# Mixture-of-experts stage of a Trainium2 kernel: experts' products of the first half of the tokens, two tiles at a time, among the projections of the second half

## The reference, cut to what matters

```
xn = layernorm(x)
logits = xn @ gate_w.T                          # 8 experts
scores = softmax(logits); weights, idx = top_k(scores, 2)
base = xn @ W_lin.T + b_lin                     # 256 -> 256
t = einsum('nd,nkdr->nkr', xn, left[idx])       # rank 4 per expert
lora = sum_k weights * einsum('nkr,nkro->nko', t, right[idx])
x = x + base + lora
```

## Time and profile before

| what | value |
|---|---|
| median of 3 runs | 5746.22 us (5745.38 to 5751.06) |
| the profiled execution: time, span | 5745.98 us, 5744.2 us |
| ffn0 | about 2289 to 2366 us of the span |
| ffn1 | about 5672 us to the end |
| PE, DVE, ACT busy over the whole span | 71%, 82%, 78% |
| granted PE clock over the whole span | 0.821 of full speed |

### The profile page before, as it was taken

One profiled execution on the slowest core, in us unless ns is written; L12 is line 12 of the kernel. 1 busy time (PEld: TensorE's weight loads), 2 busy tenths in 40 slices (PEclk: granted clock), 3 DMA queues, 4 the chain that ended last, 5 costly groups with the idle time before them and its releaser, 6 DMA issues. The chain is left out here.

```text
span 5744.2 us, 68969 instructions
## 1 busy us (share of the span) xinstructions
PE 4105.5 (71%) x22020; PEld 1826.6 (32%) x22020; DVE 4724.3 (82%) x7143; ACT 4453.8 (78%) x3416; POOL 1435.7 (25%) x1260
## 2 busy tenths in 40 slices
PE   8999999999999998855555555555555555555547
PEld 4555555555555555611111110111011111111105
DVE  7666666766666666699999999999999999999966
ACT  4555555555555555559999999999999999999994
POOL 0000000000000000034444444444444444444320
PEclk9999999999999999966667677767766676667668
DMA  1000000000000000279998989899999999999881
GB/s 40 5 6 5 5 5 5 5 5 5 5 5 5 6 6 1 79 175 189 186 198 186 198 185 198 186 198 186 197 187 198 186 198 186 198 186 198 184 193 63
DMA packets 149377, 639.49 MB, mean 111 GB/s; under 512 B 32662, under 2 KB 74840, under 8 KB 79064
## 3 DMA queue, kind: packets, MB, share of 16 engines
q0 software_dynamic: 73728, 536.90, 46.6%
q1 hardware_dynamic: 75224, 97.37, 5.1%
HBM read 70.22 MB, written 27.13 MB: 17 GB/s over the span
## 5 line engine op out<-in xcount | busy, mean ns | idle before, releaser
L1500 DVE SCALAR_TENSOR_TENSOR b_tiles<-b_ra_rep,b_cap,psum 128x1024 f32<-128x1024 f32 x1024 | 1261.0, 1271 | 56.4 <-PE psum L1761 54.1
L1761 PE MATMUL psum<-b_qT,b_kT 126*128 126x512 bf16 x2048 | 815.8, 509 | 683.7 <-DVE b_tiles L1500 680.4
L679 DVE CUSTOM_DVE_ANT_0 a_srow<-psum,a_bias 128x512 f32<-128x512 f32 (+3 forms) x1280 | 725.6, 607 | 497.6 <-PE psum L860 494.5
L738 ACT ACTIVATE a_pT<-psum 128x512 f32<-128x512 f32 (+3 forms) x1056 | 511.6, 527 | 661.0 <-PE psum L872 660.7
L1774 PE MATMUL psum<-b_tiles,b_v_aug 128*32 128x512 f32 x2752 | 524.8, 849 | 485.8 <-ACT b_tiles L1675 485.8
L1507 DVE TENSOR_SCALAR b_tiles<-b_tiles 128x2048 f32<-128x2048 f32 x512 | 767.3, 1499 | 4.4
L872 PE MATMUL psum<-ident,a_srow 128*128 128x128 f32 x4352 | 625.7, 280 | 70.5 <-DVE a_pT L551 32.9
L1666 ACT ACTIVATE b_tiles<-b_tiles 128x4096 f32<-128x4096 f32 x172 | 613.1, 3610 | 19.9 <-DVE b_tiles L1106 19.0
L756 ACT ACTIVATE a_srow<-a_srow,a_nmax 128x1536 f32<-128x1536 f32 (+15 forms) x512 | 610.3, 1197 | 23.1 <-DVE a_nmax L685 21.2
L1761 PEld LDWEIGHTS psum<-b_qT,b_kT 126*128 126x128 bf16 x2048 | 156.6, 110 | 1474.1 <-DVE b_tiles L1500 1115.2
L860 PE MATMUL psum<-a_k,a_q 64*128 64x512 f32 (+3 forms) x2560 | 624.7, 573 | 0.0
(11 more groups left out here) (221 smaller groups left out, 5242.0 us busy)
## 6 DMA issues: line engine op xcount, KB each, us to landing
b_tiles<-b_tiles POOLq DMA_DIRECT2D x344, 1024.0 KB, 13.1
X<-b_tiles POOLq DMA_DIRECT2D x168, 1024.0 KB, 13.1
b_ra_rep<-ra_scratch SPq DMA_DIRECT2D x32, 1024.0 KB, 9.9
row_scratch<-b_tiles SPq DMA_DIRECT2D x6, 2048.0 KB, 16.2
b_qk_raw<-row_scratch SPq DMA_DIRECT2D x31, 304.0 KB, 2.8
b_v_raw<-row_scratch SPq DMA_DIRECT2D x31, 136.0 KB, 8.6
X<-in_x_dram SPq DMA_DIRECT2D x8, 512.0 KB, 6.6
a_wqk<-in_wqk_dram SPq DMA_DIRECT2D x32, 128.0 KB, 2.6
```

The source lines that it names most:

```text
L679: nc.vector.tensor_tensor_reduce(out=srow[:, n % ROWS, h, a:z], in0=bank(c % 2 * 2 + h, 0, z - a), in1=bias[:, h, off + a:off + z], scale= ...
L1500: nc.vector.scalar_tensor_tensor(out=a[:, s * HALF:(s + 1) * HALF], in0=ra_rep[:, j, s * HALF:(s + 1) * HALF], scalar=cap[:, j, k:k + 1], ...
L1761: last = nc.tensor.matmul(half_ps(s)[:, i * BANK:(i + 1) * BANK], kT[:, j, k * P:(k + 1) * P], qT[:, j, cs], start=True, stop=True)
```

## The change

With HN = 8, the results n = 0 to 7 of the first half are made one by one inside the projection loop: from tile LEFT_AT = 24 on, PE issues `left_of_two(t - 24)` and `right_of_two(t - 25)` after the tile's own work, ACT copies 256 columns instead of 512, and DVE adds result t - 26 after its own work for the tile. The five parts of `choose(0)` move to the tiles 16, 17, 19, 21 and 23, and ACT's exponential to tile 16. To make room in PSUM, `joint` rotates over three banks instead of four; `left_of_two` has a bank of its own (6) and `right_of_two` two (5 and 7). The tail keeps `left` and `right` for q = 4 to 7 only, and these wait for the second half's `tl` and for the eight additions of the first half. `right_of_two(7)`, and the additions 6 and 7, stand behind the loop (the additions behind `choose(1)` too).

```diff
         def ps_joint(t, a, b):
-            return env.psum[:, (2 + t % 4) * BANK + a:(2 + t % 4) * BANK + b]
+            return env.psum[:, (2 + t % 3) * BANK + a:(2 + t % 3) * BANK + b]
...
         def ps_lora(n):
-            return env.psum[:, (2 + n % NL) * BANK:(3 + n % NL) * BANK]
+            i = (5, 7)[n % 2] if n < HN else 2 + n % NL
+            return env.psum[:, i * BANK:(i + 1) * BANK]
+        ps_tlT2 = env.psum[:, 6 * BANK:6 * BANK + 2 * P]
+        def lefts(q):
+            return HN + q - NQ // 2 + 1
...
+            def add(n):
+                dve.wait_ge(lora_done, n + 1)
+                dve.wait_ge(base_added, 2 * n + 2)
+                xt = env.X[:, 2 * n:2 * n + 2, :].rearrange("p a d -> p (a d)")
+                nc.vector.tensor_tensor(xt, ps_lora(n), xt, ALU.add).then_inc(x_added, 1)
+                if after is not None:
+                    dve.wait_ge(x_added, n + 1)
+                    after.sums(2 * n)
+                    after.sums(2 * n + 1)
...
-                if t >= HT and t % 3 == 1 and t // 3 - 5 < 5:
-                    choose(0, t // 3 - 5)
+                if t in CHOOSE_AT:
+                    choose(0, CHOOSE_AT.index(t))
+                if 0 <= t - LEFT_AT - 2 < HN:
+                    add(t - LEFT_AT - 2)
             for part in range(5):
                 choose(1, part)
-            dve.wait_ge(base_added, NT)
-            for n in range(2 * NQ):
...
+            for n in range(NT - LEFT_AT - 2, 2 * NQ):
+                add(n)
...
-                if t == HT + 1:
+                if t == HT:
                     exponentials(0)
+                n = t - LEFT_AT
+                if 0 <= n < HN:
+                    act.wait_ge(tlT_done, n + 1)
+                    if n >= 2:
+                        act.wait_ge(lora_done, n - 1)
+                    nc.scalar.activation(tlT[:, n % 2, 0:2 * P], ps_tlT2, ACT.Copy).then_inc(tlT_copied, 1)
             exponentials(1)
-            for q in range(NQ):
-                act.wait_ge(tlT_done, q + 1)
-                if q >= 2:
-                    act.wait_ge(lora_done, (q - 1) * 2)
+            for q in range(NQ // 2, NQ):
+                act.wait_ge(tlT_done, lefts(q))
+                act.wait_ge(lora_done, max((q - 1) * 2, HN))
...
                 pe.wait_ge(xT_copied, t + 1)
-                if t >= 4:
-                    pe.wait_ge(base_added, t - 3)
-                    pe.wait_ge(raw_copied, t - 3)
+                if t >= 3:
+                    pe.wait_ge(base_added, t - 2)
+                    pe.wait_ge(raw_copied, t - 2)
...
+            def left_of_two(n):
+                pe.wait_ge(tl_done, 1)
+                pe.wait_ge(ones_done, 2)
+                if n:
+                    pe.wait_ge(tlT_copied, n)
+                for i in range(2):
+                    last = nc.tensor.transpose(ps_tlT2[:, i * P:(i + 1) * P], tl[:, 2 * n + i, :], env.ident[:, :])
+                last.then_inc(tlT_done, 1)
+            def right_of_two(n):
+                pe.wait_ge(tlT_copied, n + 1)
+                if n >= 2:
+                    pe.wait_ge(x_added, n - 1)
+                for i in range(2):
+                    last = nc.tensor.matmul(ps_lora(n)[:, i * D:(i + 1) * D], tlT[:, n % 2, i * P:(i + 1) * P], ra[:, :],
+                                            start=True, stop=True, skip_group_check=True)
+                last.then_inc(lora_done, 1)
...
                 joint(t)
                 if t + 2 < NT:
                     transpose_x(t + 2)
+                if 0 <= t - LEFT_AT < HN:
+                    left_of_two(t - LEFT_AT)
+                if 0 <= t - LEFT_AT - 1 < HN:
+                    right_of_two(t - LEFT_AT - 1)
+            for n in range(NT - LEFT_AT - 1, HN):
+                right_of_two(n)
...
-            left(0)
-            for q in range(NQ):
-                if q + 1 < NQ and (q + 1) % (NQ // 2):
+            left(NQ // 2)
+            for q in range(NQ // 2, NQ):
+                if q + 1 < NQ:
                     left(q + 1)
                 right(q)
```

More of the change, by code:

```diff
@@ L122, in stage_ffn @@
     HT = NT // 2
+    HN = HT // 2
     NL = 6
+    LEFT_AT = HT + 8
+    CHOOSE_AT = [HT, HT + 1, HT + 3, HT + 5, HT + 7]
     with ExitStack() as ctx:
@@ L325, in left @@
             def left(q):
[L327 to L330, removed]
+                pe.wait_ge(tl_done, 2)
+                pe.wait_ge(tlT_copied, lefts(q) - 2)
                 for i in range(4):
@@ L335, in right @@
             def right(q):
-                pe.wait_ge(tlT_copied, q + 1)
+                pe.wait_ge(tlT_copied, lefts(q))
                 for h in range(2):
                     n = 2 * q + h
-                    if n >= NL:
-                        pe.wait_ge(x_added, n - NL + 1)
+                    pe.wait_ge(x_added, max(n - NL + 1, HN))
                     for i in range(2):
```

## The result

The changed kernel takes 5758.59 us (median of 13 runs, 5755.72 to 5763.58); the kernel before took 5746.3 us (median of 13, 5743.66 to 5751.94). The ratio is 1.0021, with a 95% interval from 1.0013 to 1.0028: it is slower, by 12.3 us. A ratio of 1 lies outside the interval, and the difference is just about the 0.2% that the prediction took for the least that can be told. Forecast were 5759 us. The profiled execution's span is 5756.6 us against 5744.2.

The account below looks back on a forecast made before the run. PE was taken to bound the projection loop. ffn1's tail 7.47, ffn0's tail 2.46 and the clock's 1.9 and 1.4 sum to +13.2 us on 5745.98, 5759.2, stated as 5759; range 5752 to 5764.

Parts of the forecast that it names:

- the price of a tile with products: Projection loop: PE takes 1.00 + 0.22 + 0.22 + 0.87 = 2.31 us for a tile with a left and a right.
- The rival that the products fit in for nothing: Projection loop: PE has room for the products, saving 6.76 us a stage, so the kernel gets faster; chance 0.05.
- Denser choosing: Projection loop: compressed choosing stalls PE for 3.2 us, net +2.6 a stage; with 6.76 for products, `base(31)` is 9.35 later.
- Three banks: Projection loop: `joint` over three banks costs nothing; if wrong, at most 0.3 us a tile.
- Tails: From the loop's end to the last addition: with the loop's delay, ffn1 ends 7.47 us later, ffn0 2.46.
- The clock behind the loop: PE idles during the second choosing, then runs 3 to 6 us at half speed: +1.9 us in ffn1, +1.4 in ffn0.
- The Trainium skill's penalty: PE's clock behind the choosing: throttled time times one half; by it ffn1 would lose 1.7 to 2.8 us.
- B: Rival: PE's clock stays up in one or both waits behind the loop; +9.9 to +11.3 us, 5756 to 5757.5; chance 0.18.
- C: Rival: compressed choosing stalls PE less in the loop; +8 us, or +4.7 without the clock's loss, 5751 to 5754; chance 0.11.
- D: Rival: products fit into the loop for nothing; 5745.7 us, or 5740.5 without the stalls too; chance 0.05.
- E: Rival: ffn0's additions hold up `right_of_two` through `x_added`, or the half-speed stretch lasts longer; over 5764 us; chance 0.04.
- The forecast's account of ffn0: ffn0: six additions (8.3 us) move into DVE's idle time and repay most of the loop's 9.35; end +2.46 without the clock.

Follow-up runs that it names:

- e7: The changed kernel with each of the eight `right_of_two` computed twice into the same place; median 5774.67 us.
- e1: The kernel before with only the denser choosing (`choose(0)` after tiles 16, 17, 19, 21, 23, exponential after tile 16), no product moved; 5748.61 us, ratio 1.0002.
- e6: The changed kernel with the products begun one tile later (LEFT_AT 25), `add(5)` still ahead of choosing; median 5757.82 us.
- e2: The kernel before with `joint` over three PSUM banks instead of four, nothing else; 5746.12 us, ratio 1.0.
- e9: The changed kernel with identity transposes filling PE's waits: 50 ahead of `left(4)`, 8 and 12 in the loop's two stalls; 5756.72 us, ratio 1.0016.
- e5: The changed kernel with 50 identity transposes on PE between `right_of_two(7)` and `left(4)`, filling the wait for the second choosing; 5759.69 us.
- e3: The change in ffn1 alone, ffn0 as in the kernel before; 5758.4 us, ratio 1.0017.
- e11: The changed kernel executed once more, unaltered, for a second profile; 5763.78 us (one run).
- e4: The change in ffn0 alone, ffn1 as in the kernel before; 5750.25 us, ratio 1.0008.
- e8: The kernel before with 44 identity transposes at the start of each mixture stage's PE program; 5743.01 us, ratio 0.9993.
- e10: The kernel before with identity transposes in PE's long waits: 32 at each mixture stage's start, 60 behind ffn0's `right(7)`, 24 at attention B; 5739.52 us, ratio 0.9988.

## Why the prediction was right

The forecast was right in its mechanism and in its sum, 5759 against 5758.59. That the sum hit within 0.4 us is luck: in the profiled executions ffn1 grew by 8.69 us where 9.4 was forecast, ffn0 by 4.26 where 3.9 was, and all the rest fell by 0.6 where nothing was. Step by step:

*What bounds the loop, and the price of a tile with products.* Forecast 2.31 us, measured 2.30, and e7 shows that PE sets it. The rival that the products fit in for nothing has fallen.

*Denser choosing.* Forecast a net 2.6 us, and with the products `base(31)` 9.35 later; measured 9.26 in ffn1 and 9.61 in ffn0. Less 6.76 for the products, 2.5 are left in ffn1. e1 gives 1.0 of them to the density, where 0.9 was forecast, and 1.5 remain for `joint(25)` behind the wait for `tl`, of which e6 takes back 1.2. The 0.35 us that ffn0 has more lie between ACT's `raws(31)` and `base(31)`; what holds DVE there is open. In e6 ffn0 does not have them (25.56 against 25.57).

*Three banks.* Nothing, as forecast (e2).

*Tails.* Without the clock ffn1 was forecast 7.47 us longer; e9 has 46.05 against 38.64, 7.41. In ffn0 2.46 was forecast, and the two parts of it that the clock leaves alone (28.22 to `base(31)` in e9, 23.18 from there in e5) give 51.40, against 48.08: 3.3. The difference is 0.35 as above and 0.50 in which `right(4)` waits for additions 6 and 7 with their sums: the forecast had weighed that wait in ffn1 only.

*The clock behind the loop.* Forecast 1.9 and 1.4 us, measured 1.28 in ffn1 and 0.95 in ffn0 (e5 against the changed kernel). The mechanism was right. The size of ffn1 is one draw: e3 lost 2.31, and the forecast lies between. The Trainium skill's penalty (TensorE: Matmul & The Clock Gate, Terms), half the throttled time, agrees: the clock was at 0.50 for about 3 us after `left(4)` in ffn1, half of which is 1.5, and some of it PE spent waiting; in e3 it was about 5 us, half of which is 2.5, against 2.31. The prediction's own figure by that rule, 1.7 to 2.8, does not follow from its 3 to 6 us, which give 1.5 to 3; nothing in the sum rests on it.

*What was missing.* The clock can also fall in the loop's own stalls, 1.4 to 1.6 us a stage, in half of the stages seen. In the profiled execution of the changed kernel it fell in neither stage, in e11 in one. How much of it is in the median is not known: the profiled execution without it took 5758.40 us, 0.2 less than the median.

*Which rival.* B, the clock staying up, is ruled out by the windows. C, that the stalls are smaller, is ruled out by 27.86. D by e7. Of E, the part on `x_added` shows only behind the loop, where `right_of_two(7)` waits 0.41 us in ffn1 and 0.76 in ffn0 for an addition; the longer stretch at half speed came in e3 and e6. The forecast's account of ffn0, six additions with their sums repaying most of the loop's growth, stands in e4: +4.27 us of 9.6.

## What to carry to other kernels

Before work is moved out of a wait into another stretch, look at both in the windows: here PE was busy 6.66 of 7.00 us where the products lay and 12.00 of 12.00 where they went, so every us moved was a us added to the loop, and only the engine that had room in the loop (DVE in ffn0) gave some back. In an engine's fixed order a wait put ahead of independent work costs that work too: with the first left one tile later the wait cost 1.2 us less, and the stages ended 0.9 us sooner. And a wait of the matrix engine has a second price behind it, its clock: cheap matmuls into a free bank, few enough that even at half clock they do not hold up the real work for long, made the unchanged kernel 0.12% faster.

## What was not expected of the hardware

The clock of the matrix engine fell not only in waits of about 5 us and more but in a pair of stalls of 0.86 and 1.47 us with two transposes between them, in five of ten stages, and in e9 across gaps of 1.13 and 0.98 us, where e5 kept it with the same gaps. The changed kernel had both outcomes in ffn0, in two executions (28.21 and 29.78 us), so the program alone does not decide over these 1.4 to 1.6 us. What does is not shown.

The clock also fell earlier or later ahead of ffn0, in attention A, whose program is the same in every kernel here. Its last four matmuls, in e11:

```profile
2288.05 2.07 PE L945 MATMUL psum<-a_wo,a_oT 128*128 128x256 f32 x4 [0.47 <-ACT a_oT L782]
```

They took 1.13 us in the profiles of before, changed, e2, e4, e6 and e7, and 2.07 or 2.08 in those of e1, e3, e5, e8, e9 and e11, with the clock at 0.50 (e10 lies between, 1.76). The first six of these executions took at most 0.4 us more than their kernel's median, the other six 3.8 to 5.8 us more. So much of the spread between executions goes together with where the clock falls in attention A. Of the difference 1.3 us lie in the start of ffn0 (25.2 to 25.3 us instead of 23.9); the rest was not followed.
